# Top-2 dispatch: full pages first by a list made on chip, the last round's row sends among the blocks

## The reference

```python
x = x + 0.5 * expert_choice(layernorm(x))   # 8 experts, each takes the 64 best tokens of a sequence, gelu
x = x + rwkv(layernorm(x))                  # scan over time
x = x + 0.5 * expert_choice(layernorm(x))
x = x + 0.5 * top2(layernorm(x))            # each token to its 2 best of 8 experts
x = x + mlstm(layernorm(x))
x = x + 0.5 * top2(layernorm(x))
```

## Time and profile before

| | us |
|---|---|
| median of 3 runs | 1747.68 |
| lowest, highest | 1744.46, 1749.17 |
| the profiled execution, its own time | 1730.8 |
| its span, first to last instruction | 1728.6 |
| TensorE busy | 1445.9 (84%) |
| VectorE busy | 1316.7 (76%) |
| GpSimd busy | 1074.2 (62%) |
| ScalarE busy | 1052.0 (61%) |

### The profile page before, as it was taken

One profiled execution on the slowest core, in us unless ns is written; L12 is line 12 of the kernel. 1 busy time (PEld: TensorE's weight loads), 2 busy tenths in 40 slices (PEclk: granted clock), 3 DMA queues, 4 the chain that ended last, 5 costly groups with the idle time before them and its releaser, 6 DMA issues.

```text
span 1728.6 us, 38821 instructions
## 1 busy us (share of the span) xinstructions
PE 1445.9 (84%) x10263; PEld 1328.4 (77%) x10263; DVE 1316.7 (76%) x3995; ACT 1052.0 (61%) x2639; POOL 1074.2 (62%) x1708
## 2 busy tenths in 40 slices
PE   8799999789958999997429999686999971099996
PEld 8589999677747999997418999685888860089996
DVE  7789999789987888887746777544788885267775
ACT  4588888545426888884126766485777730066664
POOL 7538887777743355433774666541688877746665
PEclk9899999899967999998569999856889885599998
DMA  6111010750001100100412222122222201122210
GB/s 195 50 38 32 31 36 14 179 123 1 0 2 55 39 32 32 36 8 5 151 50 63 64 65 52 39 75 76 82 79 74 78 15 47 52 63 65 63 53 10
DMA packets 93268, 96.20 MB, mean 56 GB/s; under 512 B 12073, under 2 KB 75710, under 8 KB 92577
## 3 DMA queue, kind: packets, MB, share of 16 engines
q1 hardware_dynamic: 83168, 76.70, 15.3%
q0 software_dynamic: 9920, 17.35, 3.0%
HBM read 63.75 MB, written 33.78 MB: 56 GB/s over the span
## 4 chain that ended last, share of the span: by engine, by line
PE 66%; DVE 11%; issue 9%; POOL 8%; ACT 4%; DMA 1%; DVEq 0%; POOLq 0%; ACTq 0%; SPq 0%
PE banks L600 6%; POOL rt_rows L874 5%; PE banks L589 4%; PE banks L1222 4%; PE banks L1209 4%; PE banks L580 4%; PE banks L581 3%; PE banks L582 3%; PE banks L1210 3%; PE banks L1211 3%; PE banks L1224 3%; PE banks L1223 3%; PE banks L1244 3%; PE banks L601 2%; PE banks L1194 2%
## 5 line engine op out<-in xcount | busy, mean ns | idle before, releaser
L1467 DVE TENSOR_TENSOR choice_hlo<-choice_h,choice_hhi 128x512 fp32r<-128x512 f32 x256 | 178.0, 736 | 23.2 <-ACT choice_hhi L1320 22.3
L1312 ACT ACTIVATE choice_h<-banks 128x512 f32<-128x512 f32 x256 | 152.4, 600 | 60.4 <-PE banks L1211 49.6
L833 DVE SCALAR_TENSOR_TENSOR top_h<-top_silu,top_xs,banks 128x176 f32<-128x176 f32 x364 | 128.5, 395 | 56.2 <-ACT top_silu L658 56.2
L874 POOL DMA_INDIRECT rt_rows<-X,top_slot x128 | 128.3, 1003 | 45.6 <-issue 37.2
L658 ACT ACTIVATE top_silu<-banks,top_xs 128x352 f32<-128x352 f32 x182 | 100.8, 554 | 88.3 <-PE banks L582 88.3
L1209 PE MATMUL banks<-choice_xin_hi,ec_w_hi 128*128 128x256 f32 x512 | 146.7, 286 | 4.8 <-ACT choice_xin_lo L1305 3.6
L1222 PE MATMUL banks<-choice_hhi,ec_w_hi 128*128 128x256 f32 x512 | 145.8, 285 | 2.2 <-DVE choice_hlo L1467 2.2
L1320 ACT ACTIVATE choice_hhi<-choice_h 128x512 fp32r<-128x512 f32 x256 | 146.6, 625 | 0.0
L1210 PE MATMUL banks<-choice_xin_lo,ec_w_hi 128*128 128x256 f32 x512 | 144.8, 283 | 0.0
L1211 PE MATMUL banks<-choice_xin_hi,ec_w_lo 128*128 128x256 f32 x512 | 144.6, 282 | 0.0
L1223 PE MATMUL banks<-choice_hlo,ec_w_hi 128*128 128x256 f32 x512 | 142.6, 279 | 0.0
(11 more groups left out here) (327 smaller groups left out, 5339.5 us busy)
## 6 DMA issues: line engine op xcount, KB each, us to landing
choice_token_row<-choice_tokens SPq DMA_DIRECT2D x64, 256.0 KB, 3.1
mlstm_run_row<-mlstm_run SPq DMA_DIRECT2D x32, 512.0 KB, 3.7
rt_rows<-rt_blank SPq DMA_DIRECT2D x2, 6188.0 KB, 37.9
top_xs<-rt_rows SPq DMA_DIRECT2D x182, 68.0 KB, 1.8
X<-in_x SPq DMA_DIRECT2D x8, 512.0 KB, 7.0
ec_stage<-in_ec_w SPq DMA_DIRECT2D x2, 2048.0 KB, 12.0
X<-rt_y SPq DMA_DIRECT2D x8, 512.0 KB, 6.9
rt_rows<-X,top_slot POOLq DMA_INDIRECT x128, 2.3
```

What stands on the lines that cost most here:

```text
L874: pool.indirect_dma_start(d.region[self.run], bass.IndirectOffsetOnAxis(ap=self.slot[:, t:t + 1], axis=0), self.sh.rows[:, t, :], None).th ...
L1467: dve.tensor_tensor(flat(self.hlo), self.h[:, c, :], flat(self.hhi).bitcast(F32), ALU.subtract).then_inc(self.hlo_done, 1)
```

## The change

1. `EARLY` is the last round (3). GpSimd sends only rounds 0 to 2 ahead of the blocks. The 16 sends of round 3 stand one each behind `whole` and `send` of steps 0 to 15, and count on a semaphore of their own, `sent_last`.
2. Before the last `choose`, VectorE makes a list (`arrange`), with two small matmul groups on TensorE (`arrange_sums`): the pages that are full after round 2 come first in order of number, then those that are open or not yet begun. `row_of` holds the first row of the page at each place. At least 21 pages are full by then, whatever the tokens: (8192 * 3/4 - 28 * 127) / 128 rounded up (`FULL`).
3. SyncE reads each page's row from that list into a register and loads the page at that address. Its first load waits for the list, for 48 sends and for the weights; the load at place 21 waits for `sent_last`.
4. Weights of the first top-2 layer: SyncE loads up, first and last as soon as the choice layer's up products are done, and mixed after its down products, into buffers of that layer that are dead by then. ScalarE splits the three down arrays behind the exponential of round 1, VectorE's half stands ahead of `page(1)`. The eight centred up weights stand behind `arrange`, ahead of the last `choose`, on all three engines.

```diff
+    EARLY = ROUNDS - 1
+    FULL = -(-(NT * P * EARLY // ROUNDS - PAIRS * (P - 1)) // P)
...
+    def arrange_sums(self, pe):
+        d = self.dispatch
+        pe.wait_ge(self.arranged, self.ARRANGED * self.run + 4)
+        pe.matmul(self.pplace[:, 0:1], d.upper[:, :], self.page_open[:, 0:1], start=True, stop=True)
+        pe.matmul(self.pplace[:, 1:2], d.ones[:, :], self.page_open[:, 0:1], start=True, stop=True).then_inc(self.arranged, 1)
+        pe.wait_ge(self.arranged, self.ARRANGED * self.run + 11)
+        pe.matmul(self.pplace[:, P:2 * P], self.page_number[:, :], self.page_place[:, :], start=True,
+                  stop=True).then_inc(self.arranged, 1)
...
         for r in range(self.CHOSEN_AHEAD[self.run], self.ROUNDS):
+            if r == self.EARLY:
+                self.arrange_sums(pe)
+                if not self.run:
+                    for e in range(E):
+                        centre_up(e)
             self.rank(pe, r)
-        if not self.run:
-            for e in range(E):
-                centre_up(e)
...
+            if (r, part) == (self.EARLY, "choose"):
+                self.arrange(dve)
+            if (r, part) == (self.EARLY, "choose") and not self.run:
+                for e in range(E):
+                    dve.wait_ge(sh.weights_hi, w.ups_from() + e + 1)
+                    dve.tensor_tensor(w.up_lo[:, e, :], self.pw[e % 2][:, 0:self.UP], w.up_hi[:, e, :].bitcast(F32),
+                                      ALU.subtract).then_inc(sh.weights_lo, 1)
             (self.choose_whole if part == "choose" else self.page)(dve, r)
...
-        for r in range(self.ROUNDS_AHEAD, self.ROUNDS):
+        for r in range(self.ROUNDS_AHEAD, self.EARLY):
             self.send_rows(pool, r)
...
                 whole(i, u)
             if self.block(i, u, -1):
                 send(i, u - 1)
+            if not i and u < self.RT:
+                self.send_rows(pool, self.EARLY, u, u + 1)
...
-        self.w.split.ready(sp)
-        sp.wait_ge(self.sent, 16 * NT * (self.run + 1))
+        self.w.ready(sp)
+        sp.wait_ge(self.arranged, self.ARRANGED * (self.run + 1))
+        sp.wait_ge(self.sent, 16 * self.RT * self.EARLY * (self.run + 1))
...
+            m, j = u % self.RING, self.RING * i + u
+            if j == self.FULL:
+                sp.wait_ge(self.sent_last, 16 * self.RT * (self.run + 1))
+            row = self.row_regs[j % self.PLACES]
+            sp.load(row, self.row_of[0:1, j:j + 1])
+            at = sp.snap(row, min_val=0, max_val=(self.NBLK - 1) * P)
...
-            sp.dma_start(self.xs[:, m, :], d.region[self.run][bass.ds(P * (self.RING * i + u), P), :]).then_inc(self.xs_in[m], 16)
+            sp.dma_start(self.xs[:, m, :], d.region[self.run][bass.ds(at, P), :]).then_inc(self.xs_in[m], 16)
...
-        need(sp, self.sh.x_done, self.split.after)
         sp.dma_start(self.up[:, :, :], self.sh.args["t2_up"]).then_inc(self.split.loaded, 16)
...
         if n == 3:
             self.after.gate_exp(act, 1)
+            self.after.w.split_parts(act)
...
         if n == 4:
+            self.after.w.split.rest(dve)
             self.after.page(dve, 1)
```

More of the change, by code:

```diff
@@ L2540, in build @@
                 w.up = mem.take("t2_stage_up", [P, E, Top2.UP])
[L2541 to L2543 removed]
+                before = first["choice"]
+                w.free = (before.w1_done, 2 * E * Choice.NGRP * LAYERS.count("choice"))
+                w.idle = (before.w2_done, E * Choice.NGRP * LAYERS.count("choice"))
+                assert layer.big <= before.dead_end and mem.at <= before.dead_end
+                half = before.gathered_at + 4 * E * C
+                assert half + 4 * E * C <= before.stage_at
+                w.split = Split(sh, "t2", w.parts, mem, len(choice_w.parts) + 1, choice_w.split.steps,
+                                places=(before.gathered_at, half, before.hidden_at), free=(None, None, w.idle))
+                assert mem.at <= before.hidden_end
             elif kind == "rwkv":
```

96 lines of the change are left out of this document (70 added, 26 removed).

## The result

| | before | after |
|---|---|---|
| time, median of 8 runs each | 1746.5 us (1741.2 to 1751.3) | 1759.6 us (1753.0 to 1766.0) |
| ratio | | 1.0079, 95% interval 1.0057 to 1.0102 |
| profiled execution, own time | 1730.8 us | 1763.5 us |
| its span, mean granted clock | 1728.6 us, 0.883 | 1761.6 us, 0.883 |

The change makes the kernel slower by 13 us (10 to 18 by the interval). The two profiled executions differ by 33 us.

A forecast was written before the change was run, and what follows sets the result against it. GpSimd's sends bound the fronts, TensorE the blocks at 2.09 us each. First layer -16.0 + 19.8 + 1.5 = +5.3, second -20.2 + 0.8 + 19.9 + 1.5 = +2.0; 1747.7 + 7.3 = 1755.0 us, range 1741 to 1767.

The forecast's parts named there:

- first layer, start of blocks: First top-2 layer's front: VectorE becomes the bound and the first block's start moves from 909.62 to 893.6, minus 16.0 us.
- second layer, start of blocks: Second layer's front: GpSimd's 48th send starts 20.2 us earlier than its last did; SyncE's register load adds 0.8 us.
- first layer, up to the 22nd: First layer's blocks: the 22nd waits for the 16 sends behind the blocks, at 63.6 us against 43.8, plus 19.8 us.
- second layer, up to the 22nd: Second layer's blocks: the same wait at the 22nd block, at 63.2 us against 43.3, plus 19.9 us.
- idle of TensorE at the 22nd: One TensorE idle before the 22nd block's turn, 18 to 22 us in each layer; under 14 us would be wrong.
- cold restart, 22nd copy to 22nd add: After the stall at the 22nd block TensorE's clock will have fallen: 1.5 us a layer, ends 0 and 2.5.
- VectorE's front is longer: First layer's front, list of 8 us or weights or ScalarE late: gains 8 instead of 16, 1763 us; chance 0.12.
- The rival in which VectorE locks the row sends among the blocks: Each of 16 sends behind blocks meets a 0.7 us lock: 10 us more in each layer, 1776 us; chance 0.05.
- The register load: SyncE's new register load from SBUF ahead of each block load: 0.8 us, between 0 and 1.23.
- SyncE's pace: SyncE's new load sets the pace in all 91 blocks: 24 us on top at 1.8 us each, 1779; chance 0.03.
- the gaps that close: GpSimd's gaps close among the blocks: step 2.55 us, stall 13 us a layer, 1741.5 us; chance 0.12.
- the wait that does not bind: The wait at block 22 does not bind: both stalls and their clock cost go, 1712 us; chance 0.03.

The follow-up runs named there:

- where no load waits: Changed kernel; second-layer blocks load from the first layer's region, the 16 sends stay behind the blocks but no block load waits for them: 1746.0 us, ratio 1.0026.
- all waited for: Changed kernel with all 64 row sends ahead of GpSimd's first add and SyncE waiting for all before its first load: 1748.1 us, ratio 1.0021.
- no sends in the second layer's blocks: Changed kernel; second-layer blocks load from the first layer's region, its last 16 sends left out, no wait at block 22: 1725.3 us, ratio 0.9904.
- additions in their place: Changed kernel; second-layer blocks load from the first layer's region, its last 16 sends each replaced by a GpSimd addition: 1726.1 us, ratio 0.9909.
- 8 spaced, 8 behind: Changed kernel with 8 last-round sends ahead of the first add, each waiting for a TensorE turn, and 8 behind blocks 0 to 7: 1721.3 us, 0.9874.

## Why the prediction was right in the sum and wrong in its parts

Forecast +7.3 us, 1755.0, range 1741 to 1767, slower; measured 1759.6, +13.1 (10 to 18). The direction, its reason (the last round's sends behind the blocks give back more than the fronts bring) and the place of the wait were right. By two of its own signs of being wrong it failed all the same: TensorE's idle time at the 22nd block is under 14 us in both layers, and the first layer starts after 898. Against the traces:

| step | predicted | measured |
|---|---|---|
| first layer, start of blocks | -16.0 us | -12.3 us (mean second turn 903.6 in five traces, 915.9 in two of before) |
| second layer, start of blocks | -20.2 and +0.8 | -21.4 (477.3 in five traces, 498.7 in two) |
| first layer, up to the 22nd | +19.8 | +22.9 (65.2 in five traces, 42.3 in two) |
| second layer, up to the 22nd | +19.9 | +24.4 |
| idle of TensorE at the 22nd | 19.8, 19.9 | 7.8, 9.1 and 8.4, 9.9 |
| slower blocks ahead of it | 0 | second layer: 13.6 and 16.4 in the two traces of after, 17.7 where no load waits |
| cold restart, 22nd copy to 22nd add | 1.5, 1.5 | +2.3, +2.4 |

The five traces are those of kernels whose first layer is the changed one, and for the start of the second layer the same five. With the cold restart (the 22nd add stands 25.1 us further behind the second turn than before in the first layer) the first layer loses 12.8 us and the second, by its two traces, 4.1: 16.9 in the traces, 13.1 in the medians. The 16.9 are 9.6 more than forecast: the two stretches up to the 22nd block give 7.5 of it, the first front 3.7, the restarts 1.6, and the second front, 22.6 us in the two traces of after, takes 3.2 off. That the two fronts missed in opposite directions is luck.

**The front of the first layer.** This is the term of a front that failed: -16.0 was set against a trace of before without a single releaserless wait, and such waits hit both kernels there. The -12.3 beside it rests on two traces of before that lie 11.7 us apart, so its size is uncertain by several us. In the second trace of after VectorE's work reads: slots of the third round at 865.97 (862.95 predicted), list 5.5 us (4.5), centred weights 10.0 (9.9), last choice and paging 18.8 (16.1, with 4.93 of it a releaserless wait), first subtract at 900.21 (893.6). Its terms were sized well where VectorE ran free, and it was the bound, as said. In the first trace of after 5.12 and 2.34 us on ScalarE and 4.32 and 2.80 on VectorE brought it to 912.23. That is the rival "VectorE's front is longer", with another mechanism than a slow list.

**The give-back.** "From there a step is add 0.47, gap 0.17 or 0.30, write 0.99, gap 0.30, row send 0.96" held: 2.94. What failed is that TensorE runs its 21 blocks at 2.09 us meanwhile. The wait at the 22nd block is the difference between two chains; since the blocks slow beside the sends, TensorE arrives there 14 to 18 us later and waits less for it. That the sum came out near is no luck here: GpSimd's chain, which was forecast, sets the time of the 22nd turn whichever engine waits. GpSimd's chain is itself lengthened when blocks come late (the last row send 52.4, 52.0, 49.3 and 50.0 us after the first add in the four cases, 46.1 predicted), so the end moved by 3 to 4.5 us a layer more. A forecast of the idle time alone would have been read as wrong by half, though the 22nd turn came nearly when forecast.

**The rival in which VectorE locks the row sends among the blocks** fell: all sends there take 0.96 to 0.99 us. The opposite happened, the sends held up the others. The lock by the weight subtracts was seen again where it was put: the sends beside the 2.33 and 3.88 us subtracts took 1.47 and 4.64 us and were hidden by the wait of 4.81 us for slots. The Trainium skill, SBUF — State Buffer, section on the two separate sides, says that a VectorE instruction with two SBUF inputs and a GpSimd one that reads SBUF exclude each other on a shared port pair; both rows agree.

**The register load.** Predicted 0.8 us in 0 to 1.23; its median is 0.27 and the loads' spacing grew by 0.34 (16 in 12.59 us, 7.45 before) in the first layer and 0.40 in the second. The Trainium skill, DMA: Bandwidth & Descriptors, latency table, has a floor of about 0.6 us for it; both 0.27 and 0.40 lie under it, so the measurement decides. Beside back-to-back sends the same instruction took 1.40.

**SyncE's pace, the gaps that close, the wait that does not bind**: none came. The moved weights change the median by nothing that can be measured (0.9978 to 1.0011).

## What to carry to other kernels

Moving a producer's last sends behind the consumer's first work pays only if the sends fit into the producer's spare time; here 0.3 to 0.4 us a block stood against 1.26 us a send, and idle time that was free (GpSimd's 16 and 32 us before the first add) lay right beside it. And a send costs more than its own time: 16 of them slowed the blocks by 17.7 us with no load waiting for them. Put part of the sends into the idle time, spaced where that is free: 8 in the fill and 8 behind the blocks made 1721 us out of 1744, the best of the study (1724 back to back, not clearly different), where 16 behind the blocks made 1760. And profile the kernel before twice when its profiled time lies outside its timed runs: one clean trace hid the effect on which the front's term failed.

## What the runs showed that was not expected

While GpSimd issues indirect sends close together (1.3 to 1.7 us from one to the next), other engines of the core wait without a cause in the trace. It was seen in 13 of 14 traces, always between 780 and 1000 us or 1500 and 1620 us, where row sends run or have just ended; none of 14 traces has such a row before 780, from 1010 to 1400 or after 1620, though output sends run there, one per 2.1 us. Sums of such idle time ("remote" alone), VectorE and ScalarE together:

| kernel | front, 780 to 903 | first blocks, 903 to 1000 | second layer, 1500 to 1620 |
|---|---|---|---|
| before, two traces | 0, 43.1 | 0, 0 | 0, 0 |
| all waited for | 7.9 | 0 | 0 |
| weights moved only | 25.0 | 0 | 0 |
| after, two traces | 22.3, 12.3 | 13.8, 11.9 | 12.2, 13.5 |
| no sends in the second layer's blocks | 7.9 | 11.8 | 0 |
| additions in their place | 9.9 | 13.7 | 0 |
| 8 spaced, 8 behind | 5.3 | 6.5 | 5.2 |

A send has to be near for it, but is not enough: in the front of the second layer (1440 to 1500) sends run too, and no trace names such a wait. In both places a time of 1.40 us comes back: the longest register load and the longest plain issue of SyncE, the spacing of VectorE's starts at 886.32, 887.72 and 889.12, and that of the ends of TensorE's idle times at 1500.59, 1501.99 and 1503.38.

The waits are not spread evenly over the instructions either. In six traces one of 2.0 to 5.8 us stands at the same instruction of VectorE (the reciprocal L779 of the last round), at 889 to 893, around the end of the sends. In nine of the twelve traces with moved weights one of 1.7 to 4.4 us stands at ScalarE's copy of the eighth centred weight (L666), at times from 878 to 895. What the other engines share with the sends, and whether the place in an engine's program matters or only the moment, no run here tells apart. Left open, too, is why the weights' move costs nothing although the slots come later.
